# Both gather sums on a ring of 128 tile slots, with the forward message weights freed ahead of them

## What is computed

```python
ht = jnp.einsum('ne,reh->rnh', hidden, weights[l])          # 18 = 2 x 9 relations
msg_f = ht[edge_type, src] + biases[l][edge_type]
out = segment_sum(msg_f, dst, num_segments=n_nodes)
msg_b = ht[edge_type + n_rel, dst] + biases[l][edge_type + n_rel]
out = out + segment_sum(msg_b, src, num_segments=n_nodes)
```

## Time and profile before

| | us |
|---|---|
| median of 3 runs | 5438.61 (5426.68 to 5443.8) |
| the profiled execution | 5436.53 |
| its span on the core | 5434.8 |
| mean granted clock of TensorE | 0.694 |

### The profile page before, as it was taken

One profiled execution on the slowest core, in us unless ns is written; L12 is line 12 of the kernel. 1 busy time (PEld: TensorE's weight loads), 2 busy tenths in 40 slices (PEclk: granted clock), 3 DMA queues, 4 the chain that ended last, 5 costly groups with the idle time before them and its releaser, 6 DMA issues. The chain is left out here.

```text
span 5434.8 us, 50013 instructions
## 1 busy us (share of the span) xinstructions
PE 3062.4 (56%) x13750; PEld 2237.6 (41%) x13751; DVE 2231.2 (41%) x2709; ACT 614.3 (11%) x1076; POOL 3413.0 (63%) x3213
## 2 busy tenths in 40 slices
PE   3899989567777777744918633343333333333333
PEld 1788879233333333324917422232222323232223
DVE  7999985445555454568901331111111111101112
ACT  0455540000000000004701000000000000000000
POOL 2888868466556555657770356666666666666664
PEclk7999999666666666657958766665665656555555
DMA  5566667144444444425825332222222111111111
GB/s 177 157 181 192 177 198 230 37 131 138 132 133 139 132 135 130 139 87 159 259 62 195 136 100 70 69 64 60 60 59 60 48 46 46 45 46 46 46 46 46
DMA packets 498663, 599.91 MB, mean 110 GB/s; under 512 B 190115, under 2 KB 367441, under 8 KB 496248
## 3 DMA queue, kind: packets, MB, share of 16 engines
q0 software_dynamic: 117856, 246.12, 16.5%
q1 hardware_dynamic: 337751, 229.77, 14.8%
q10 hardware_dynamic: 42944, 122.68, 6.0%
HBM read 406.69 MB, written 204.36 MB: 112 GB/s over the span
## 5 line engine op out<-in xcount | busy, mean ns | idle before, releaser
L720 POOL DMA_INDIRECT rec_by_src<-rec,pos x782 | 1123.3, 1436 | 524.6 <-issue 238.9
L1132 PE MATMUL ps<-g_got,g_hot 128*128 x3224 | 687.5, 367 | 1225.8 <-issue 797.4
L1132 PEld LDWEIGHTS ps<-g_got,g_hot 128*128 128x128 f32 x3224 | 605.7, 272 | 1320.2 <-issue 1318.9
L1592 POOL DMA_INDIRECT sc_kv<-kv,d_src x806 | 761.8, 945 | 533.9 <-DVE sc_kve L1644 260.2
L1032 POOL DMA_INDIRECT g_got<-y_forward,d_msg x782 | 739.3, 945 | 381.8 <-issue 230.1
L1032 POOL DMA_INDIRECT g_got<-y_back,s_msg x782 | 737.8, 943 | 381.2 <-issue 233.5
L805 PE MATMUL ps<-ln_low,ln_hot 128*125 128x256 f32 x2848 | 620.3, 381 | 20.3 <-DVE ln_low L782 16.1
L805 PEld LDWEIGHTS ps<-ln_low,ln_hot 128*125 128x125 f32 x2848 | 535.6, 188 | 104.8 <-issue 24.4
L1043 DVE TENSOR_TENSOR g_hot<-ps,src_loc 128x1024 f32<-128x1024 f32 x101 | 120.6, 1221 | 992.5 <-remote 450.4
L1699 PE MATMUL ps<-w_e,sc_attrT 128*128 128x512 f32 x404 | 320.0, 887 | 246.0 <-ACT sc_attrT L1611 216.3
L1051 DVE TENSOR_TENSOR g_y<-ps,ms_b 128x384 f32<-128x384 f32 x75 | 41.8, 558 | 808.8 <-remote 474.2
(11 more groups left out here) (323 smaller groups left out, 3283.7 us busy)
## 6 DMA issues: line engine op xcount, KB each, us to landing
linked<-ln_out SPq DMA_DIRECT2D x320, 224.0 KB
ve<-sc_kve ACTq DMA_DIRECT2D x202, 256.0 KB
wv_ve<-ve SPq DMA_DIRECT2D x101, 512.0 KB
l_links<-linked SPq DMA_DIRECT2D x25, 800.0 KB
l_links<-linked ACTq DMA_DIRECT2D x25, 800.0 KB
f_links<-linked SPq DMA_DIRECT2D x25, 800.0 KB
f_links<-linked ACTq DMA_DIRECT2D x25, 800.0 KB
attr_pairs<-ln_feats POOLq DMA_DIRECT2D x7, 2048.0 KB
```

Source lines behind the costliest of these rows:

```text
L720: pool.indirect_dma_start(out=dram["rec_by_src"], out_offset=bass.IndirectOffsetOnAxis(ap=S["pos"][:, c:c + 1], axis=0), in_=S["rec"][:, c ...
L1132: last = pe.matmul(ps[:, bass.ds(columns[j], width)], hot[:, q, j, :], got[:, bass.ds(slots[j], width)], start=False, stop=True, skip_grou ...
L1592: pool.indirect_dma_start(out=kv[:, q, j, :], out_offset=None, in_=dram["kv"], in_offset=bass.IndirectOffsetOnAxis(ap=S["d_src"][:, c:c + ...
```

## The change

Four things, all in one diff:

1. `SLOTS` is 128, so `RING` is 16: `got` has twice the size, POOL waits for pair group g - 13 from group 16 on, the seven index gathers of g3 stand ahead of tile group 24, there are 16 landing semaphores, and the loops of g4 hold 16 groups (6 passes and 5 groups after them, where it was 12 and 5).
2. Weights and biases are held in halves: `mf_w`, `mf_b` for the forward messages, freed before the gather sums, and `mb_w`, `mb_b` for the backward ones, kept through g3. SP loads them with four DMAs, and those who wait for them wait for 64.
3. `y`, where g3 stages its rows, lies in the buffer `skip`, which the earlier stages are done with.
4. The part of the step tables at width `AW` is dropped; the other two move up. An unused option of `linked_sum` goes too.

```diff
-SLOTS = 64
+SLOTS = 128
 RING = SLOTS // GROUP
...
-        self.steps_of = 2 * pair_blocks + SPLIT_BLOCKS if self.windows else 3 * pair_blocks
+        self.steps_of = 2 * pair_blocks + SPLIT_BLOCKS if self.windows else 2 * pair_blocks
...
-                    link(dve.tensor_scalar_mul(steps[:, 0:blocks], s.held[:, :], float(AW)))
-                    link(dve.tensor_scalar_mul(steps[:, blocks:2 * blocks], s.held[:, :], float(D)))
+                    link(dve.tensor_scalar_mul(steps[:, 0:blocks], s.held[:, :], float(D)))
...
-            y = m.sb(tag + "_y", [P, 2, HW])
+            y = S["skip"][:, 0:2 * HW].rearrange("p (k w) -> p k w", k=2)
...
-                for n, (source, factor) in enumerate(((s.held, AW), (s.held, D), (s.blk, D))):
-                    link(dve.tensor_scalar_mul(s.columns[:, n * s.blocks:(n + 1) * s.blocks], source[:, :], float(factor)))
+                for n, source in enumerate((s.held, s.blk)):
+                    link(dve.tensor_scalar_mul(s.columns[:, n * s.blocks:(n + 1) * s.blocks], source[:, :], float(D)))
...
-            sp.dma_start(S["ms_w"][:, :].rearrange("p (r h) -> p r h", h=D), weights[last].rearrange("r e h -> e r h")).then_inc(S["ms_loaded"], 16)
-            sp.dma_start(S["ms_b"][:, :], biases[last].rearrange("(a r) h -> a (r h)", a=1).to_broadcast([P, RW])).then_inc(S["ms_loaded"], 16)
+            for name, lo, hi in (("mf", 0, RELATIONS), ("mb", RELATIONS, 2 * RELATIONS)):
+                sp.dma_start(S[name + "_w"][:, :].rearrange("p (r h) -> p r h", h=D), weights[last][lo:hi].rearrange("r e h -> e r h")).then_inc(S["ms_loaded"], 16)
+                sp.dma_start(S[name + "_b"][:, :], biases[last][lo:hi].rearrange("(a r) h -> a (r h)", a=1).to_broadcast([P, HW])).then_inc(S["ms_loaded"], 16)
...
-            pe.wait_ge(S["ms_loaded"], 32)
+            pe.wait_ge(S["ms_loaded"], 64)
```

More of the change, by code:

```diff
@@ L47 @@
 RELATIONS = 9
-RW = 2 * RELATIONS * D
 HW = RELATIONS * D
@@ L526, in climb_of @@
                 else:
-                    link(dve.tensor_scalar_mul(steps[:, 0:blocks], s.held[:, :], float(AW)))
-                    link(dve.tensor_scalar_mul(steps[:, blocks:2 * blocks], s.held[:, :], float(D)))
+                    link(dve.tensor_scalar_mul(steps[:, 0:blocks], s.held[:, :], float(D)))
                     link(dve.tensor_scalar(s.part_i[:, :], s.tile_i[:, :], SLOTS - 1, None, ALU.bitwise_and))
-                    link(dve.tensor_copy(steps[:, 2 * blocks:], s.part_i[:, :]))
-                    link(dve.tensor_scalar_mul(steps[:, 2 * blocks:], steps[:, 2 * blocks:], float(D)))
+                    link(dve.tensor_copy(steps[:, blocks:], s.part_i[:, :]))
+                    link(dve.tensor_scalar_mul(steps[:, blocks:], steps[:, blocks:], float(D)))
                 dve.engine_nop().then_inc(stepped, 1)
@@ L842, in _, with linked_sum @@
                 sp.wait_ge(saved[r], 64 * (SPLITS // REGIONS + 1))
-def linked_sum(nc, S, dram, tag, which, weights=None, biases=None):
+def linked_sum(nc, S, dram, tag, which):
     WAYS = 4
@@ L1125, in landed_group @@
                 q = k % WAYS
-                columns = load_columns(nc, S, mybir.EngineType.PE, name, 1, start_of(i, k))
-                slots = load_columns(nc, S, mybir.EngineType.PE, name, 2, start_of(i, k))
+                columns = load_columns(nc, S, mybir.EngineType.PE, name, 0, start_of(i, k))
+                slots = load_columns(nc, S, mybir.EngineType.PE, name, 1, start_of(i, k))
                 pe.wait_ge(heated[q], i * (RING // WAYS) + (k // WAYS + 1))
@@ L1144, in rows_of @@
                         pe.wait_ge(biased, b * PIECES + k)
-                    pe.matmul(area, S["x_t"][:, b * D:(b + 1) * D], S["ms_w"][:, HW + k * PIECE:HW + (k + 1) * PIECE],
+                    pe.matmul(area, S["x_t"][:, b * D:(b + 1) * D], S["mb_w"][:, k * PIECE:(k + 1) * PIECE],
                               start=True, stop=True).then_inc(product, 1)
@@ L1686, in step @@
                 _, cols = nc.values_load_multi_w_load_instructions(
-                    S["dst_steps"][0:1, bass.ds(start + PAIR_COLS, STEP)], engines=[mybir.EngineType.PE], min_val=0,
+                    S["dst_steps"][0:1, bass.ds(start, STEP)], engines=[mybir.EngineType.PE], min_val=0,
                     max_val=(BLOCKS - 1) * D, skip_runtime_bounds_check_because="block numbers are counts of blocks")
@@ L2138, in _ @@
                         pe.wait_ge(biased, n - AREAS + 1)
-                    pe.matmul(area(n), S["x_t"][:, b * D:(b + 1) * D], S["ms_w"][:, k * PIECE:(k + 1) * PIECE],
+                    pe.matmul(area(n), S["x_t"][:, b * D:(b + 1) * D], S["mf_w"][:, k * PIECE:(k + 1) * PIECE],
                               start=True, stop=True).then_inc(product, 1)
@@ L2278, in gnn_kernel @@
             S["d_msg"], S["s_msg"] = (r.sb(n, [P, TILES], I32) for n in ("d_msg", "s_msg"))
-            S["src_steps"] = r.sb("src_steps", [1, 3 * PAIR_COLS], I32)
+            S["src_steps"] = r.sb("src_steps", [1, 2 * PAIR_COLS], I32)
             with ExitStack() as third:
                 t = Memory(nc, third)
-                S["ms_w"], S["ms_b"], S["x_t"] = (t.sb("ms_" + n, [P, width]) for n, width in (("w", RW), ("b", RW), ("xT", ROWS)))
+                S["mb_w"], S["mb_b"], S["x_t"] = (t.sb(n, [P, width]) for n, width in (("mb_w", HW), ("mb_b", HW), ("ms_xT", ROWS)))
                 S["ms_loaded"] = t.sem("ms_loaded")
-                mlp_and_linked_sum(nc, S, dram, ins["L3_gnn_weights"], ins["L3_gnn_biases"])
-                norm_and_messages(nc, S, dram)
+                with ExitStack() as fore:
+                    f = Memory(nc, fore)
+                    S["mf_w"], S["mf_b"] = f.sb("mf_w", [P, HW]), f.sb("mf_b", [P, HW])
+                    mlp_and_linked_sum(nc, S, dram, ins["L3_gnn_weights"], ins["L3_gnn_biases"])
+                    norm_and_messages(nc, S, dram)
                 gather_sum(nc, S, dram, "g3", "dst", tables[0], S["d_msg"], back=True)
```

16 lines of the change are left out of this document (6 added, 10 removed).

## The result

| | before | after |
|---|---|---|
| median | 5433.44 us (4 runs, 5426.68 to 5443.8) | 5477.94 us (4 runs, 5471.05 to 5483.45) |
| span of the profiled run | 5434.8 | 5469.3 |
| mean granted clock of TensorE | 0.694 | 0.691 |

The changed kernel takes 1.0083 times as long, 95% interval [1.0069, 1.0098]. It was forecast at 5215 and is 263 us above that, on the other side of no change.

The account below looks back on a forecast made before the run. POOL's issue of 2 x 782 gathers, with its waits for PE's sums, was taken as the bound. 5436.5 - 130.8 (back sum) - 130 (forward sum) + 40 (ends) = 5215.7, rounded to 5215 us; range 5155 to 5320.

Parts of the forecast that it names:

- The waits go, -276.0: Both gather sums: POOL's waits on `summed`, 276.0 us, go if PE keeps up; taken as -130 forward, -130.8 back.
- A fast stretch lasts while PE has dense work: PE in the gather sums: a crawl doesn't end a catch-up early, and waiting groups take 2 to 4 us each.
- Ends of the sums, +40: End of each gather sum: the last landing may fall into a PE crawl, +20 us for each sum.
- The edits costed at nothing: Weights in halves, row staging in the skip buffer, dropped tables: nothing; at most 6.6 us for the weights without SP's spare.
- SP's bias loads: End of SP's list: each half's bias costs 5.68 us, +6.6 with the second weight issue, within 15.5 us spare.
- The seven row gathers: Forward sum, before tile group 24: start near 3390, keep 8.7 us of POOL, cost nothing, or 10 us without cover.
- C: Rival, chance 0.07: PE is at its limit at six groups a cycle, POOL finishes early, nobody gains, 5430 us.
- E: Rival, chance 0.06: steady supply lengthens PE's crawls; at 5.5 groups per 68.3 us, 5538 with the back sum alone.
- D: Rival, chance 0.06: back sum's longer loop leaves PE's instruction window; 18 fetches at 2 us, 36 us, 5215 to 5250.

Follow-up runs that it names:

- experiments 6: Changed kernel with POOL's lead 3 in the forward sum and 13, 8, 3, 2 by stretch in the back sum: 5428.29 us, kernel before 5405.28.
- experiment 8: Changed kernel with leads 3, 5 and 13 in both sums, on one chip with crawls: 1.0013, 1.0000 and 1.0081 of the kernel before.
- experiment 3: Two variants of the changed kernel's back sum: six more matmuls per group, 5512.25 us; moving slots at fixed columns, not from registers, 5469.54 us.
- Experiment 1: Changed kernel with SLOTS back at 64, its other edits kept: 5421.33 against 5419.17 us for the kernel before, ratio 1.0007.
- experiment 7: Changed kernel, forward lead 8; back sum with 128-byte rows for groups 33 to 65 and asked-for POOL pauses from group 66: 5460.45 us.
- (2): Changed kernel, but the back sum gathers only its first 128 tiles and PE sums the later groups without waiting for landings: 4765.63 us.
- h1: Changed kernel, but in the back sum SP loads plain rows and POOL is idle, on a chip without crawls: 4057.41 us.

## Why the prediction was wrong

**The waits go, -276.0 (in the sum -130 and -130.8): the step that failed.** POOL's time moved by -6.6 and +3.6. The premise was that these waits go if PE keeps up on average, and its proof the 314.1 and 109.0 us in which PE waited for landings. Keeping up isn't enough. At lead 3 PE waited 720.1 us for landings in g4 and had each sum soon after its rows, and POOL still stood still for 134.0 us, since the news of the sums came up to 20 us late, and that of three groups in four only when POOL was silent (experiments 6 and 8). Nor was the idle time spare. With 13 groups of lead PE gave up those waits and crawled instead: it waited 31.2 us and still summed a group per 11.4 us. At every lead POOL's pauses made 124 to 143 us of each sum, about 1.3 to 1.5 us a group of gathers. A pause isn't a stock running out, which a deeper ring would cover. It is the time in which PE and the news of its sums come right: of some twenty crawls of g4 after the change, fifteen end 3 to 6 us after POOL falls silent, and the first 19 us after. My own rows hinted at it: a catch-up began with POOL's pause, beside the earlier trace rows, though the pause before that one had brought DVE a single sum and left the crawl as it was the earlier trace rows. I read it as PE letting POOL go, and asked only what PE could do in it.

**"A fast stretch lasts while PE has dense work": wrong.** It rested on one burst in g3. In g4 after the change PE has landed groups waiting nearly all the time, and most fast stretches end 11 to 14 us after POOL resumes.

**Ends of the sums, +40: right in sign, low.** It was +54.8 (35.6 in g3, 19.2 in g4), and for another reason. I priced one crawl that a last landing might meet. What there was is PE's whole backlog, 11 to 14 groups at 2 to 3.5 us each, after POOL has stopped; in experiment 3, with a dearer group, 75.5 us. Before the change the backlog could be no more than five groups, and at the end of these sums PE had caught up. This term alone is the result: with POOL's pauses as they were, the deeper ring brought only its depth, paid once at the end of each sum.

**The edits costed at nothing: right.** Experiment 1 has them together at 1.0007. SP's bias loads took 2.92 and 2.95 us, not 5.68 each:

```profile
2988.45 2.92 SPq L1353 DMA_DIRECT2D mf_b<-in_L_gnn_biases_dram  x1
...
2991.89 2.95 SPq L1353 DMA_DIRECT2D mb_b<-in_L_gnn_biases_dram  x1
```

The seven row gathers start at 3400.9 (3390 was reckoned), and DVE reads them at 3524.0, over 100 us later, so it didn't stand waiting for them.

**Rivals.** C was nearest in number, 5430. Its sign was to be POOL finishing with PE over ten groups behind, and that came: 176 matmul records, eleven groups, stand after POOL's last start in g4 (60 before the change). It got 0.07, for the 314.1 us against it. But POOL didn't finish early, as C had it, PE wasn't at its limit (experiment 8), and C lacked the tail. E had the sign of the result, slower, to which 0.06 was given, and a part of the mechanism: POOL's pause is what lets PE drain, and crawls do lengthen (31 us of 68 before, 40 of 57 after, 112.1 and more the first). But its step from there to far fewer groups per us was wrong; the cycle shortened with them, to 11.4 us a group from about 11.2. D, the loop that no longer stays in PE, wanted 18 instruction blocks in g4, at a price of 2 us each that no row gave. The queues from 4400 to 5400 show two:

```profile
q8 instruction: 2, 0.03, 0.0%
```

By the rule of the Trainium skill ("Runtime: NRT & Kernel Launch", "Instruction fetch mechanics") on a window of two blocks, a body of 2.9 blocks (the prediction's estimate) would be fetched anew in each pass. This trace doesn't agree: two packets in 1000 us, some five passes.

**What stays open.** Why PE and the news of its sums slow down while POOL gathers, and why on some chips alone. The runs rule out the number of bytes (experiment 7), the slots' registers (3) and a pattern of PE's own work (2), each by one run. Why PE's matmuls crawl at leads of 5 and more and not at 3, while the news is late at all of them, isn't shown either. The runs don't tell POOL's issuing of gathers from the transfers that follow. Loads issued by something other than POOL might; they ran only on a chip without crawls (h1). Pauses of POOL that don't hang on PE might too, but those didn't take effect (7).

## What to carry to other kernels

A consumer's idle time isn't proof of spare capacity: where it alternates with a slow phase, ask what the producer was doing in both, before a deeper buffer is priced by it. And a producer that waits for a sum waits for the news of it: compare when the consumer's work was through with when the others went on. Where that news comes late while the producer is at work, no depth of the ring need remove the pauses; here none of four did. A deeper ring then only moves the backlog to the end of the stage, where it is paid at depth times the consumer's fast time per item (here tails of 32 to 48 us against 12 to 18, twice). Price a ring first by its tail.

## What the chip showed that I hadn't expected

- While POOL issues indirect gathers one after the other, PE on some chips at times goes on at one matmul record per 2.80 us (granted clock 0.50) when it has groups waiting (leads 5, 8 and 13). With the gathers left out it returned, 16 us after the last one, to 2.7 us for a group, at 0.98. At lead 3 PE never crawled.
- On those chips the news of most finished sums reaches DVE late at every lead, at lead 3 up to 20 us. There DVE and POOL mostly go on together, once POOL has been silent for 5 to 6 us. On the others it takes under 0.2 us.
- The same kernel takes 5405 to 5433 us on one kind of chip and 4655 to 4662 on the other. In the profiles of the changed kernel about 485 us of that lie ahead of the gather sums (the forward gathers start at 3133.0 and at 2647.5), and the rest in them.
- POOL's pace of an indirect gather of 128 rows is 1.248 us, for rows of 512 and of 128 bytes alike.
